# Cross-attention in a Perceiver layer: the output projection of the pair behind, and its addition to the residual, one step of keys later

## What is computed

```python
def _L0_xattn_ref(query, key, value, w_q, w_k, w_v, w_o):    # HEADS = 16, HEAD_DIM = 64, HIDDEN = 256
    q = (query @ w_q).reshape(B, Q, HEADS, HEAD_DIM).transpose(0, 2, 1, 3)
    k = (key @ w_k).reshape(B, Kl, HEADS, HEAD_DIM).transpose(0, 2, 1, 3)
    v = (value @ w_v).reshape(B, Kl, HEADS, HEAD_DIM).transpose(0, 2, 1, 3)
    scores = jnp.einsum('bhqd,bhkd->bhqk', q, k) * scale
    attn = jax.nn.softmax(scores, axis=-1)
    out = jnp.einsum('bhqk,bhkd->bhqd', attn, v)
    return out.transpose(0, 2, 1, 3).reshape(B, Q, HEADS * HEAD_DIM) @ w_o

x = x + _L0_xattn_ref(_layernorm(x, axis=-1), ctx_1024, ctx_1024, ...)
x = x + _L0_attn_ref(_layernorm(x, axis=-1), ...)
x = x + _L0_ffn_ref(_layernorm(x, axis=-1), ...)
```

## Time and profile before

| | |
|---|---|
| median of three runs | 1398.77 us |
| profiled execution | 1400.91 us |
| its span on the core | 1398.7 us |
| mean granted TensorE clock over the span | 0.957 of full speed |

### The profile page before, as it was taken

How to read it: one execution, slowest core, us unless ns; L and a number is a source line. 1 busy time by engine, 2 the same in 40 slices (tenths; PEclk the granted TensorE clock), 3 DMA queues, 4 the chain that set the end, 5 groups by cost and what they waited for, 6 DMA issues and landing times. The chain is left out here.

```text
span 1398.7 us, 21065 instructions
## 1 busy us (share of the span) xinstructions
PE 1257.7 (90%) x8379; PEld 939.1 (67%) x8379; DVE 879.3 (63%) x1042; ACT 723.3 (52%) x1304; POOL 411.8 (29%) x372
## 2 busy tenths in 40 slices
PE   3999999999999999899999999999999697969533
PEld 2786877777786868587868687777778443636312
DVE  5647676766766676547676767676776456513576
ACT  3655556565656556546565655655565231523152
POOL 3605051433425150414342505152342102211010
PEclk9999999999999999999999999999999798979776
DMA  4303020302021133210311203030202354250000
GB/s 154 76 1 74 7 80 1 80 1 80 18 63 50 28 78 93 74 36 2 79 42 39 60 22 79 1 80 1 76 3 63 129 95 55 35 57 1 23 0 15
DMA packets 42528, 68.19 MB, mean 49 GB/s; under 512 B 5040, under 2 KB 31152, under 8 KB 42432
## 3 DMA queue, kind: packets, MB, share of 16 engines
q1 hardware_dynamic: 40896, 66.21, 19.3%
q10 hardware_dynamic: 1536, 0.66, 0.4%
HBM read 25.89 MB, written 0.52 MB: 19 GB/s over the span
## 5 line engine op out<-in xcount | busy, mean ns | idle before, releaser
L455 DVE TENSOR_REDUCE step_max<-score_banks 128x2 f32<-128x1024 f32 x256 | 300.5, 1221 | 122.2 <-PE score_banks L579 122.2
L476 DVE TENSOR_TENSOR prob_sum<-prob_sum,probs 128x1024 f32<-128x1024 f32 x224 | 279.4, 1288 | 139.5 <-ACT probs L406 138.8
L338 POOL TENSOR_TENSOR k_split<-probs,k_split 64x512 fp32r<-64x512 f32 x128 | 163.6, 1278 | 327.6 <-ACT probs L389 323.7
L406 ACT ACTIVATE probs<-score_banks 128x1024 f32<-128x1024 f32 x181 | 181.9, 1028 | 149.4 <-PE out_ps L605 85.3
L593 PE MATMUL score_banks<-q_twice,k_split 128*128 128x256 f32 x724 | 182.2, 288 | 0.2 <-ACT probs L406 0.2
L594 PE MATMUL score_banks<-q_low_max,k_ones 128*128 128x256 f32 x724 | 178.1, 283 | 0.0
L340 POOL TENSOR_TENSOR k_split<-probs,k_split 64x512 fp32r<-64x512 f32 x128 | 163.9, 1281 | 9.6
L593 PEld LDWEIGHTS score_banks<-q_twice,k_split 128*128 128x128 f32 x724 | 138.3, 191 | 11.9 <-issue 6.2
L594 PEld LDWEIGHTS score_banks<-q_low_max,k_ones 128*128 128x128 f32 x724 | 138.5, 191 | 0.0
L331 POOL TENSOR_TENSOR w_lo<-w_raw,w_hi 128x768 fp32r<-128x768 f32 x16 | 36.2, 2260 | 336.5 <-ACT w_hi L357 336.5
L381 ACT ACTIVATE k_split<-key_banks 64x512 fp32r<-64x512 f32 x128 | 75.5, 590 | 104.7 <-PE key_banks L542 104.1
(11 more groups left out here) (207 smaller groups left out, 2169.2 us busy)
## 6 DMA issues: line engine op xcount, KB each, us to landing
k_ones<-k_split SPq DMA_DIRECT2D x128, 256.0 KB, 4.0
ctx_rows<-in_ctx_dram SPq DMA_DIRECT2D x10, 512.0 KB, 3.8
grouped_far<-dots_far SPq DMA_DIRECT2D x32, 136.0 KB
w_raw<-in_L_xattn_w_v_dram SPq DMA_DIRECT2D x14, 256.0 KB, 3.5
probs<-in_ctx_dram SPq DMA_DIRECT2D x6, 512.0 KB, 5.9
w_raw<-in_L_xattn_w_q_dram SPq DMA_DIRECT2D x16, 128.0 KB, 3.5
w_raw<-in_L_xattn_w_k_dram SPq DMA_DIRECT2D x16, 128.0 KB, 3.8
wo_pair<-in_L_xattn_w_o_dram SPq DMA_DIRECT2D x16, 128.0 KB, 2.1
```

The costliest lines, as they stand in the source:

```text
L338: pool.tensor_tensor(k_split[DH:P, A, keys], keys_staged[j % 2][0:DH], k_split[0:DH, A, keys].bitcast(F32), ALU.subtract).then_inc(k_low[A ...
L406: act.activation(probs[:, j % 2, h, :], scores_of, ACT.Exp, scale=SCALE).then_inc(exp_done, 1)
L455: dve.tensor_reduce(step_max[:, qt, :, j], score_banks[:, 2 * qt:2 * qt + 2, :], X, ALU.max).then_inc(max_done, 1)
L476: dve.tensor_tensor(prob_sum[:, h, :], prob_sum[:, h, :], probs[:, j % 2, h, :], ALU.add).then_inc(sum_done, 1)
```

## The change

`project_output` of the pair behind moves from turn 4 to turn 5 of PE's loop, and `add_output` from behind the maxima of step 2 to behind those of step 3 in DVE's stream. Nothing else differs.

```diff
@@ DVE, body of a pair
                     if j == 1 and it > 0:
                         divide(it - 1)
-                    if j == 2 and it > 0:
+                    if j == 3 and it > 0:
                         add_output(it - 1, last_batch(b, i))
@@ PE, body of a pair
                     if j == 2 and it > 0:
                         sum_over_keys(it - 1)
-                    if j == 4 and it > 0:
+                    if j == 5 and it > 0:
                         project_output(it - 1)
                     if values_behind(i, j) is not None:
                         project_v(it, b, i, parity, values_behind(i, j))
```

## The result

| | median of the runs | ratio to the kernel before, 95% interval |
|---|---|---|
| kernel before | 1399.57 us (1397.69 to 1403.32, 5 runs) | |
| changed kernel | 1433.86 us (1432.34 to 1444.78, 5 runs) | 1.0254 (1.0228 to 1.028) |

The change costs 34.3 us, 2.5%; 1434.0 was forecast. In a later set one execution was disturbed throughout (2476.55 us) and is left out, with its profile.

A forecast was written before the change was run, and what follows sets the result against it. PE's stream, busy 90% of the span, was taken as the bound. Ordinary pairs 28.4 - pair 8 1.2 + clock 8.0 = 35.2 us, on the median 1398.8 gives 1434.0 us; range some 1422 to 1449 us.

The forecast's parts named there:

- The ordinary pair: Pairs 1 to 7 and 9 to 15: value piece waits about 1.65 us for the addition; 2.03 us longer each, 28.4 us.
- Nothing is won back: After the value piece, PE's streams only shift; its remaining wait of 0.16 us at 200.68 recovers at most 2.2 us.
- SP: SP's copies into `k_ones` shift with the projection's end, 2.7 us later, hidden behind 5 us.
- Pair 8: Piece 1 comes a turn later, so the addition stays covered and the value piece starts earlier: 1.2 us gained.
- The clock: PE's granted clock falls after the new waits in 5 of 14 pairs, at 1.60 us each: 8.0 us lost.
- The share of one in three: One of three long PE waits was followed by the low clock; the same share gave 5 of 14 pairs.
- The clock holding in all pairs: Rival: 0 to 2 falls of PE's clock, 1426.0 to 1429.2 us; chance 0.30.
- The low clock in most pairs: Rival: PE's clock falls in 9 to 14 pairs, 1440.4 to 1448.4 us; chance 0.15.
- Absorption: Rival: the 2.03 us a pair goes into a later wait of PE, about 1399 us; chance 0.05.
- gain: Rival: PE's wait for the quotient goes and nothing replaces it, 11.2 us saved, 1387.6 us; chance 0.03.

The follow-up runs named there:

- second profile of the changed kernel: The changed kernel run again unchanged, one execution with its profile: 1437.77 us.
- experiment 4: Changed kernel plus twelve matmuls whose result nothing reads, behind the projection in the 14 pairs whose value piece waits: 1426.49 us, ratio 1.0181.
- second set: The changed kernel measured again unchanged, beside other kernels of the same call: 1432.94 us, ratio 1.0234.
- experiment 2: Kernel before with DVE's half alone: addition behind the maxima of step 3, projection still in turn 4: 1466.62 us, ratio 1.0476.
- first profile of the changed kernel: Profiled execution of the unchanged changed kernel in the first measurement, the slowest of its five: 1444.78 us.

## Why the prediction was right

The forecast, its mechanism and its sum held: 34.3 us measured, 35.2 reckoned.

- *The ordinary pair.* 2.03 was reckoned, 1.99 measured (66.04 against 64.05), from the same steps: keys at once, two waits for the maxima, the projection, a wait to 0.78 + 1.65 behind the projection's start (2.43 in the trace, and 2.44 in the sum: 193.07 - 190.63). What had to be seen is that DVE, idle for 122.2 us in all, is the late one at this place.
- *Nothing is won back.* Right: the keys, scores and value pieces behind are shifted as a whole; the wait of 0.16 at 200.68 is 0.17 now.
- *SP.* Right: its sixth and seventh copy into `k_ones` moved with the projection, and the seventh is still bound by the last keys, as in the earlier trace rows:

```profile
197.47 1.04 SPq L308 DMA_DIRECT2D k_ones<-k_split  x1
202.61 0.46 SPq L307 DMA_DIRECT2D k_ones<-k_split  x1
```

- *Pair 8.* From its scores at 611.40 to the value piece at 617.00 it takes 5.60, before 6.82: 1.22 gained, 1.2 reckoned. Two details of the reckoning were wrong, without effect. The staging copy at 583.63 is that of key step 4, not 3, so the keys didn't wait for it; the maxima set the time anyway. And a batch's first pair makes two value pieces in turn 5, not one in turn 5 and one in turn 6 as the kernel's description ahead of the prediction has it; the second goes into `out_ps` right behind the first, whose 1.5 us just cover the addition:

```profile
616.22 1.13 PE L622 MATMUL out_ps<-wo_pair,outT 128*128 128x256 f32 x4
617.00 0.59 PE L562 MATMUL v_ps<-w_hi,ctxT_lo 128*128 128x256 f32 x2
...
618.64 0.44 PE L562 MATMUL out_ps<-w_hi,ctxT_lo 128*128 128x128 f32 x2
```

  But the gain is the clock's. The 6.82 hold the fall that cost 1.60, and the sum took the new order at the full clock without saying so. In this profile no fall came, and the pair is 1.0 shorter than before. In the second profile of the changed kernel the clock fell at the value piece, and pair 8 took 77.79 us (589.47 to 667.26), 0.4 longer than the 77.38 before.

- *The clock.* 8.0 us reckoned, 6 to 8 measured (34.3 less the 26.2 of experiment 4; 5.9 with the second set's 32.1). The size is right, the make-up is coarser: falls in 2 or 3 of 12 ordinary pairs at 1.3 to 1.6 us, where 5 of 14 at 1.60 stood, and longer ones in the last pair of a batch, which no row of the kernel before showed. The share of one in three was luck in part. It was taken from three waits, while the earlier trace rows has a fourth, 2.32 us long to 1101.72, within which the clock fell:

```profile
1100.00:1101.00 1.00, 0.00 (x0) 0.00 (x0) 1.00 (x1) 0.00 (x0) 0.00 (x0) 0.94 0.02 8
1101.00:1102.00 1.00, 0.28 (x1) 0.28 (x2) 0.64 (x2) 0.00 (x0) 0.00 (x0) 0.50 0.00 0
```

  With two falls in four waits the same step would have given 7 x 1.60 = 11.2 us and a forecast of 1437.2.

The rivals fell as follows. The clock holding in all pairs is what experiment 4 made by hand, and its 1426.5 is the 1426.0 of that rival. The low clock in most pairs is what experiment 2 has, with a wait of 2.81 instead of 1.65. Absorption and gain are out by the waits of PE.

The Trainium skill, page "TensorE: Matmul & The Clock Gate", section "Why this matters for your kernels", warns, for drops in mid-kernel, of idle gaps longer than any single gap in these pairs. The runs differ: waits recorded as 1.3 us were followed by 1.2 GHz in two or three ordinary pairs of 12, those of 2.8 us in 11 of 12, those of 0.8 us in none.

## What to carry over

A step that is moved later on one engine can come to stand right ahead of the next writer of its buffer; then the reader's whole queue on the other engine lies on the path, however idle that engine is on average. Count what stands between producer, reader and next writer in every stream, before and after. To hide a short wait, independent work (here a value piece in another bank) in front of the waiting instruction served better than moving the waiting instruction behind other waits: 0.28 us less a pair against 2.0 more, and 0.75 less with both once the buffers were apart. And a bubble on PE may cost more than its length: 1.65 us of waiting, repeated 14 times, took 6 to 8 us more through the clock, and useless matmuls in the bubble gave them back.

## What was not expected of the hardware

The clock can stay low although PE is busy. In the first profile of the changed kernel it lay at 0.51 over the 31 us from 526 us, with PE busy for 30.87 of them, in the last pair of the first batch; in ordinary pairs it was back about three microseconds after the fall, as in the earlier trace rows. What PE did there differs in one thing that I could see: the last pairs' value pieces have 128 columns where the others have 256, and the scores of the second phase, of 256, had begun at 554.82 when the clock rose. But in the last pair of the second batch it rose after some ten microseconds, still among such pieces. In the second profile of the changed kernel the two last pairs had 10 and 3 us, in experiment 2 they had 7 and 31. Whether these pieces are the cause was not tried. Nor is it settled why of pairs with the same waits some lose the clock and some don't.
